# Second layer's query stacks transposed by DMA, maxima split and masks on GpSimd, rounding products on ScalarE

## What is computed

```
x += attention(layernorm(x), context, mask)      # 16 heads; masked scores; softmax over 128 keys; output product
x += feed_forward(layernorm(x))
layer 0: products of rounded activations (127 steps of the row's largest value) and ternary weights; tanh form of silu(gate) * up, rounded again, down
layer 1: gate logits, the best 2 of 8 experts, two fp32 products per expert, weighted sum
```

## Time and profile before

| | |
|---|---|
| time, median of 3 runs | 215.11 us (214.87 to 216.59) |
| the profiled execution's own time | 216.64 us |
| its span, first to last instruction | 214.8 us |
| TensorE (PE) busy | 196.6 us, 92% |
| VectorE (DVE) busy | 162.4 us, 76% |
| ScalarE (ACT) busy | 135.3 us, 63% |
| GpSimd (POOL) busy | 82.7 us, 38% |
| mean granted clock of TensorE | 0.987 of full speed |

### The profile page before, as it was taken

How to read it: one execution, slowest core, us unless ns; L and a number is a source line. 1 busy time by engine, 2 the same in 40 slices (tenths; PEclk the granted TensorE clock), 3 DMA queues, 4 the chain that set the end, 5 groups by cost and what they waited for, 6 DMA issues and landing times.

```text
span 214.8 us, 6119 instructions
## 1 busy us (share of the span) xinstructions
PE 196.6 (92%) x2114; PEld 160.8 (75%) x2114; DVE 162.4 (76%) x608; ACT 135.3 (63%) x378; POOL 82.7 (38%) x197
## 2 busy tenths in 40 slices
PE   2487697999999999999999999999999999999992
PEld 0255474757766777777888988898979889999992
DVE  6458989999999999999987859966576736265225
ACT  3343466468868677766968579547955576566430
POOL 4494320432337544143520425438210604232532
PEclk9999889999999999999999999999999999999998
DMA  5849678504440724430080000400220000000000
GB/s 156 243 111 303 164 98 349 145 9 101 108 92 0 160 50 92 98 87 17 2 92 9 5 0 17 98 3 12 54 47 6 0 15 0 17 0 15 2 10 24
DMA packets 39747, 15.09 MB, mean 70 GB/s; under 512 B 34211, under 2 KB 38819, under 8 KB 39462
## 3 DMA queue, kind: packets, MB, share of 16 engines
q1 hardware_dynamic: 39142, 14.00, 27.7%
q10 hardware_dynamic: 576, 0.72, 1.0%
HBM read 5.80 MB, written 0.52 MB: 29 GB/s over the span
## 4 chain that ended last, share of the span: by engine, by line
PE 81%; DVE 7%; DMA 5%; issue 2%; SPq 2%; POOL 1%; ACT 1%; DVEq 0%; ACTq 0%
PE ps_B L826 14%; PE ps_A L839 12%; PE ps_O L756 7%; PE ps_B L690 7%; PE ps_A L675 6%; PE ps_B L692 6%; PE ps_Q L708 6%; PE ps_A L677 6%; DMA m0T_i<-in_mask0T 5%; PE ps_O L764 3%; PE ps_X L722 2%; PE ps_A L791 2%; PE ps_O L774 2%; PE ps_A L835 2%; PE ps_P L736 2%
## 5 line engine op out<-in xcount | busy, mean ns | idle before, releaser
L907 ACT ACTIVATE probs<-ps_B 128x512 f32<-128x512 f32 x64 | 36.5, 598 | 15.6 <-PE ps_B L692 14.8
L956 ACT ACTIVATE hid<-ps_B,b_sb 128x128 f32<-128x128 f32 x128 | 35.6, 378 | 15.3 <-PE ps_B L826 15.2
L1063 DVE TENSOR_REDUCE mx<-ps_A 128x4 f32<-128x512 f32 x64 | 42.0, 677 | 3.7 <-PE ps_A L677 3.7
L826 PE MATMUL ps_B<-mxT,w_sb 128*128 128x128 f32 x256 | 33.3, 278 | 0.0
L839 PEld LDWEIGHTS ps_A<-w_sb,hid 128*128 128x128 f32 x256 | 31.1, 192 | 0.6
L839 PE MATMUL ps_A<-w_sb,hid 128*128 128x128 f32 x256 | 31.2, 275 | 0.0
L826 PEld LDWEIGHTS ps_B<-mxT,w_sb 128*128 128x128 f32 x256 | 30.6, 192 | 0.5 <-issue 0.4
L654 POOL TENSOR_TENSOR yc<-yc 128x512 f32<-128x512 f32 (+2 forms) x21 | 17.3, 823 | 34.1 <-DVE yc L1228 33.0
L675 PE MATMUL ps_A<-m_b,id_b 128*128 128x512 bf16 x64 | 24.7, 385 | 2.4 <-DVE mx L1063 1.2
L692 PEld LDWEIGHTS ps_B<-qmT,kblk 118*128 118x128 bf16 x256 | 20.4, 100 | 8.6 <-issue 0.8
L692 PE MATMUL ps_B<-qmT,kblk 118*128 118x128 bf16 x256 | 25.5, 223 | 0.0
(11 more groups left out here) (135 smaller groups left out, 391.5 us busy)
## 6 DMA issues: line engine op xcount, KB each, us to landing
w_sb<-in_m1T SPq DMA_DIRECT2D x1, 1024.0 KB, 6.2
w_sb<-in_m2T SPq DMA_DIRECT2D x1, 1024.0 KB, 8.1
out_y<-out_sb SPq DMA_DIRECT2D x8, 64.0 KB, 1.5
x_sb<-in_x SPq DMA_DIRECT2D x1, 448.0 KB, 6.7
ctx_sb<-in_ctxT ACTq DMA_DIRECT2D x1, 448.0 KB, 5.5
m_i<-in_mask SPq DMA_DIRECT2D x1, 384.0 KB, 4.2
m0T_i<-in_mask0T SPq DMA_DIRECT2D x1, 384.0 KB, 5.0
kblk<-kst SPq DMA_TRANSPOSE x16, 3.7
```

The costliest lines, as they stand in the source:

```text
L826: mm = pe.matmul(psum("z", b, i)[:, c * P:(c + 1) * P], w1_sb[:, 4 * i + c, :], mxT[:, b % 2, :], start=True, stop=True)
L907: ends(act.activation(probs[:, n % 2, 4 * i:4 * i + 4, :], psum("exp", n, i)[:, :].rearrange("p (h k) -> p h k", h=4), ACT.Exp, scale=ATTN ...
L956: ins = act.activation(hid[:, b % 2, 4 * i + c, :], psum("z", b, i)[:, c * P:(c + 1) * P], ACT.Relu, bias=b1_sb[:, 4 * i + c:4 * i + c + 1])
L1063: ends(dve.tensor_reduce(mx[:, n % 2, 4 * i:4 * i + 4], psum("max", n, i)[:, :].rearrange("p (h k) -> p h k", h=4), AX.X, ALU.max), "dve.max")
```

## The change

1. In layer 1 the query stack is turned by two DMA transposes on SP's queue (`sp.qs`, `sp.qb`) in place of sixteen TensorE transposes and two ScalarE copies. Layer 0 keeps TensorE. The buffers `qst`, `qT` and `qmT` get 4, 3 and 3 slots (before 3, 2, 2).
2. The split of the maxima runs on GpSimd (`p1`, `pr`, `p2`, `p3`) in both layers; the reduction itself negates its result. The masks of layer 0 are made on GpSimd.
3. The multiply-and-add of the three roundings (`xr`, `hr`, `wa`) runs on ScalarE.
4. The masks are loaded in three pieces (2, 2 and 4 sequences), the expert weights in four pieces each, behind the fourth to seventh key transposes; layer 1's small tensors go one key transpose later.
5. Units (0,6) and (0,7) come ahead of (1,1), and the due times are all new, with six values per unit in place of one. To make room, `th` and `hr` lie in the buffer of the weights, and the bias buffers in `yc`.

```diff
+QSLOTS = 4
+TSLOTS = 3
+MSLOTS = 3
+BY_DMA = (1,)
...
-UNIT_ORDER = ((0, 0), (0, 1), (0, 2), (0, 3), (0, 4), (0, 5), (1, 0), (1, 1), (0, 6), (0, 7), (1, 2),
+UNIT_ORDER = ((0, 0), (0, 1), (0, 2), (0, 3), (0, 4), (0, 5), (1, 0), (0, 6), (0, 7), (1, 1), (1, 2),
...
+QUERY_STACK = ((("pe.qs", 1, "pool.ql"), ("act.qs", 1, "pe.qs")),
+               (("sp.qs", 1, "pool.ql"),))
+SHIFTED_STACK = ((("pe.qb", 1, "pool.p3"), ("act.qb", 1, "pe.qb")),
+                 (("sp.qb", 1, "pool.p3"),))
...
                 if n == 0:
                     sp.dma_start(wo_sb[0][:, :], w0o).then_inc(s_wo, 16)
+                    masks(1, 2, 4)
                 if n == 1:
-                    masks(1, 2, NB)
...
                 if n == 2:
+                    masks(2, 4, NB)
...
+                if n in (3, 4, 5, 6):
+                    part = slice(4 * (n - 3), 4 * (n - 3) + 4)
+                    sp.dma_start(w1_sb[:, part, :], m1T[:, part, :]).then_inc(s_moe, 16)
+                    sp.dma_start(w2_sb[:, part, :], m2T[:, part, :]).then_inc(s_moe, 16)
...
+                if name == "qs":
+                    after(sp, "pool.ql", n)
+                    if n >= TSLOTS:
+                        after(sp, "pe.max", n - TSLOTS)
+                    if b >= 2:
+                        wait_landed(sp, b - 2, "qs")
+                    sp.dma_start_transpose(qT[:, n % TSLOTS, :, :], qst[:, n % QSLOTS, :, :].rearrange("p g c -> p (g c)")
+                                           ).then_inc(landed["qs"][b % 2], 16)
+                if name == "qb":
+                    after(sp, "pool.p3", n)
+                    if n >= MSLOTS:
+                        after(sp, "pe.exp", n - MSLOTS)
...
+                if name == "mk":
+                    if b in (0, 2, 4):
+                        for src in s_mask[b:b + 2]:
+                            pool.wait_ge(src, 16)
+                    pool.tensor_scalar(m0_b[:, b, :], m0_i[:, b, :], 0.0, MASKED, ALU.is_equal, ALU.mult)
+                    ends(pool.tensor_scalar(m0T_b[:, b, :], m0T_i[:, b, :], 0.0, MASKED, ALU.is_equal, ALU.mult), "pool.mk")
+                if name == "p1":
+                    st, m, rest = head_max(n)
+                    after(pool, "dve.max", n)
+                    ends(pool.tensor_copy(st[:, :, :, 0], m), "pool.p1")
+                if name == "pr":
...
+                    ends(pool.tensor_tensor(rest, m, st[:, :, :, 0], ALU.subtract), "pool.pr")
+                if name == "p2":
...
+                    ends(pool.tensor_copy(st[:, :, :, 1], rest), "pool.p2")
+                if name == "p3":
...
+                    ends(pool.tensor_tensor(st[:, :, :, 2], rest, st[:, :, :, 1], ALU.subtract), "pool.p3")
...
+            def query_stack_ready(n):
+                if units[n][0] in BY_DMA:
+                    wait_landed(pe, units[n][1], "qs")
+                else:
+                    after(pe, "act.qs", units[n][1])
...
+                if name == "hr":
+                    after(act, "dve.h3", b)
...
+                    ends(act.activation(hr[:, :], z2[:, b % 2, :], ACT.Copy, bias=ROUND, scale=fs[:, b, 11:12]), "act.hr")
+                if name == "xr":
...
+                    ends(act.activation(xr[:, b % 2, :], fh[:, 0, b % 2, :], ACT.Copy, bias=ROUND, scale=fs[:, b, 3:4]), "act.xr")
+                if name == "wa":
...
-                                           psum("max", n, i)[:, :].rearrange("p (h k) -> p h k", h=4), AX.X, ALU.max),
-                         "dve.max")
...
+                                           psum("max", n, i)[:, :].rearrange("p (h k) -> p h k", h=4), AX.X, ALU.max,
+                                           negate=True), "dve.max")
```

More of the change, by code:

```diff
@@ L118 @@
     ("dve.fn", 1, "pool.fp"),
-)
+) for l in range(2)]
 STEPS = (
-    (("dve.mk", 1),) + ATTENTION + (
+    (("pool.mk", 1),) + ATTENTION[0] + (
         ("dve.q0", 1, "dve.fn"),
@@ L262, in steps_of @@
+GROUP = {name: k for k, names in enumerate(STAGES) for name in names.split()}
 def steps_of(n):
@@ L287, in ready @@
             if n >= ring:
-                needs.append((reader, n - ring, parts[0][reader] - 1))
+                if reader == "stack.qb":
+                    reader = SHIFTED_STACK[UNIT_ORDER[n - ring][0]][0][0]
+                needs.append((reader, n - ring, (parts[0].get(reader) or parts[1][reader]) - 1))
         for ring, reader in LAYER_SLOTS[l].get(name, ()):
@@ L291, in ready @@
                 needs.append((reader, number[l, b - ring], parts[l][reader] - 1))
+        if name in ("sp.qs", "sp.qb") and b >= 2:
+            needs.append((name, number[l, b - 2], 0))
         if name in AFTER_LAYER0 and l == 1:
             needs.append(("dve.dn", number[0, b], 0))
-        if name in AFTER_KEYS and b >= AFTER_KEYS[name][0]:
-            needs.append(("sp.ks", AFTER_KEYS[name][1], 0))
+        needs += [("sp.ks", k, 0) for first, k in AFTER_KEYS.get(name, ()) if b >= first]
         if b == 0:
@@ L412, in build @@
         b1_sb = sb("b1_sb", [P, ZCH])
-        b2_sb = sb("b2_sb", [P, E * P])
-        b2_f = sb("b2_f", [P, E * P])
+        yc = sb("yc", [P, 2, E, P])
+        b2_sb, b2_f = [yc[:, i, :, :].rearrange("p e o -> p (e o)") for i in range(2)]
         b2_h = sb("b2_h", [P, E * P], BF16)
@@ L482, in build @@
         bank_zero, last_out_ready, last_sum = sem("bank_zero"), sem("last_out_ready"), sem("last_sum")
-        ks_landed = [sem("ks_landed0"), sem("ks_landed1")]
+        landed = {k: [sem(f"{k}_landed{i}") for i in range(2)] for k in ("ks", "qs", "qb")}
         s_out = [sem("out_stored0"), sem("out_stored1")]
@@ L885, in _ @@
                     after(act, "pe.q", n)
-                    if n >= 3:
-                        after(act, "pe.qb", n - 3)
+                    if n >= QSLOTS and units[n - QSLOTS][0] in BY_DMA:
+                        wait_landed(act, units[n - QSLOTS][1], "qb")
+                    elif n >= QSLOTS:
+                        after(act, "pe.qb", units[n - QSLOTS][1])
                     elif n:
@@ L1172, in _ @@
                     ends(dve.tensor_scalar(f(11), f(10), QMAX, f(5), ALU.mult, ALU.mult), "dve.h3")
[L1173 to L1177 removed]
                 if name == "hq":
[L1179 removed]
+                    after(dve, "act.hr", b)
                     if b >= 2:
```

276 lines of the change are left out of this document (131 added, 145 removed), and 7 rows, old and new, of the table START.

## The result

The changed kernel is slower: 218.32 us median of 4 runs (217.79 to 220.15) against 214.99 for the kernel before, a ratio of 1.0171 with an interval of 1.0135 to 1.0208. The forecast was 204.4 us, so 13.9 us are to be explained, and the measured time lies outside the forecast's range of 195 to 214.5 us.

The account below looks back on a forecast made before the run. TensorE's work was taken as the bound behind 75 us, with VectorE also near full before. From 216.64 us, -7.2 - 4.3 + 0.8 = -10.7 gave 205.9; less 1.53 to the median, 204.4 us, range 195 to 214.5.

Parts of the forecast that it names:

- 16 stacks off TensorE: Layer 1, nearly all behind 75 us: 16 stacks at 0.45 us leave TensorE, whose work is the time there; -7.2 us.
- VectorE's relief, masks at the start: Ahead of 75 us: VectorE's relief closes TensorE gaps, -4.3 us; first masks on GpSimd delay the start, +0.8 us.
- The new order is not costed: All engines' lists: with TensorE full, a new order can change only gaps already counted; 0 us.
- The second rival: GpSimd paces layer 0: splits waiting for maxima hold the next unit's parts; 214.6 us, no change to measure; chance 0.10.
- The -4.3 ahead of 75 us: Ahead of 75 us: relieving VectorE wins back two thirds of TensorE's recoverable 6.4 us; -4.3 us.
- Its own sign of being wrong: From 20 to 40 us: TensorE still starving, not under 2 us idle, or dropping to the lower clock level.
- the 6.4 us: TensorE's recoverable time before 75 us: idle 3.46 and 1.26 us, plus 1.7 us lost to slow clock at 25 to 29.
- 1.53 us above the median: Whole kernel: the profiled execution's 216.64 us lies 1.53 us above the runs' median; taken off the forecast.
- Landings at 0: Layer 1: query stacks land 0.8 to 2.7 us later by DMA, covered by expert products; 0 us.
- a landing at the front of TensorE's list: TensorE's list: a wait for a landing at its front while expert products stand behind it would show the forecast wrong.
- ScalarE's part near 0: ScalarE: 9.5 us of copies leave, at most 11 us of rounding products come; about even, 0 us.

Follow-up runs that it names:

- run 6: The kernel before with layer 1's sixteen query stacks left out altogether, neither on TensorE nor by DMA, every other step's order unchanged: 212.73 us.
- 15: The changed kernel with GpSimd's list reordered, the bias load one key transpose earlier, and layer 1's sixteen stacks left out altogether: 211.35 us.
- run 11: The changed kernel with seven steps of GpSimd's list in other places and the bias load one key transpose earlier: 212.51 us.
- run 9: The changed kernel with only seven steps of GpSimd's list in other places, no work added or removed: 213.18 us.
- run 2: The changed kernel with layer 1's stacks back on TensorE and ScalarE, all other lists as they are: 221.6 us.
- 7: The changed kernel with layer 1's sixteen stacks left out altogether, no DMA transposes and nothing in their place: 216.95 us.
- run 1: The kernel before with layer 1's query stacks turned by DMA, with 4, 3 and 3 slots, other lists as before: 218.39 us.
- 8: The kernel before with the split of the maxima alone moved to GpSimd, right behind each unit's maxima: 215.43 us.
- run 16: The kernel before with layer 1's stacks left out altogether and the split of the maxima on GpSimd: 212.18 us.
- run 12: The changed kernel with GpSimd's list reordered, the bias load earlier, and four parts of score products moved in TensorE's list: 214.23 us.

## Why the prediction was wrong

The terms of the sum along one path of steps from the kernel before to the changed one, in medians of runs:

| term | forecast | measured | from |
|---|---|---|---|
| 16 stacks off TensorE | -7.2 | -2.3 | before against 6 (215.05, 212.73) |
| VectorE's relief, masks at the start; measured: all else of the change, with GpSimd's list mended | -3.5 | -1.4 | 6 against 15 (211.35) |
| landings of the DMA transposes | 0 | +1.2 | 15 against 11 (212.51) |
| the bias block's place | 0 | +0.7 | 11 against 9 (213.18), ranges overlap |
| the new order of GpSimd's list | 0 | +5.1 | 9 against the changed kernel (218.32) |
| sum | -10.7 | +3.3 | |

A price depends on the lists around it: in the changed ones the stacks on TensorE cost 221.6 - 216.95 = 4.7 us (runs 2 and 7), not 2.3. The rounding products on ScalarE, the loads in pieces, the unit order and the due times were not run by themselves; they are in the -1.4.

- **"The new order is not costed: with TensorE full it can change only the gaps already counted. 0 each."** This step failed by most, 5.1 us for GpSimd's list and up to 5.8 with the bias load, and it turned the sign: run 11 without it lies under the kernel before. Ahead of 75 us TensorE was not full, and the order decides there what it waits for. I priced the work that GpSimd got (1.36 us for two masks, 1.24 for a split; both came out about so) and not its place in a list that is served in order. The second rival named the mechanism ("a split waiting for maxima holds the next unit's parts") and priced it at no change, 214.6 us, 3.7 below what was measured; it had a chance of 0.10. The mask behind such a split is the case.
- **"There TensorE's amount of work is the time" behind 75 us, -7.2 in full.** The work did leave, but run 6 shows that only 2.3 us of it come off when the order of every other step stays. That TensorE was busy for 133.65 of 133.8 us says that it ended last, not by how much: the next chains were 2.3 us behind. The quarter of the stretch that other engines had to spare is no measure of that either, since a chain of dependent steps needs no full engine.
- **The -4.3 ahead of 75 us.** Its own sign of being wrong came: from 20 to 40 us TensorE stands idle for 3.63 us (forecast under 2) at a granted clock of 0.91 (forecast full). Two things were wrong with it. VectorE's relief was 10.0 us, not 22.1, since groups' busy times overlap: from 20 to 75 us VectorE is busy for 46.2 of 55 us, 84%, where the forecast had about 70 (its own rows give 64). And 1.7 of the 6.4 us was the half clock of 25 to 29 us, which the other profiled executions with nearly the same lists there do not have: runs 1, 6, 8 and 16 were granted 1.00 in that stretch. The same execution lay 1.53 us above the median, which I took off too. If the half clock is what set it apart, the two thirds of 1.7 us that are in the -4.3 were counted twice. Where VectorE did come down, from 20 to 40 us, TensorE waited for GpSimd's list in its place. What the relief is worth by itself no run shows.
- **Landings at 0.** Lists that plan for them hide most (1.2 us); lists that do not pay 218.39 - 212.73 = 5.7 us (run 1 against 6, which has fewer slots). The wait that I named as the sign of being wrong, a landing at the front of TensorE's list, is there (2.0 us in two waits), but run 12 shows that moving it back does not win it. The Trainium skill's rule to turn a 128x128 block on TensorE where PSUM will do as the destination (VectorE: DVE Perf Modes, "Rules for kernel authors") is borne out in the old lists, where the DMA is 3.8 us slower (run 1), and not in the changed ones, where it is 3.3 us faster than the stacks on TensorE (run 2).
- **Right:** the work moved (TensorE 190.9 us, GpSimd 108.9), and ScalarE's part near 0: of the waits listed only one of 0.9 us, for `hq`, lies behind a rounding product.

**Still open** is what holds the 4.9 us of the first term. It is not the landings (run 6 has none), and taking the split off VectorE gives at most 0.5 (run 16). Run 6's chain of waits speaks for most of it lying ahead of 114 us, in chains through VectorE. That the order of TensorE's own list keeps it is a guess; a list made anew for the shorter work was not tried.

## What to carry to other kernels

A chain that is all one engine tells who ends last, not how far the next is behind; leave the work out altogether and measure before you book its whole price as a gain. When steps go to an engine that serves a list in order, read what stands behind each of them and what each waits for: here seven steps in another order were worth 5.1 us, more than the 2.3 and 1.4 us that the moves brought. And a disturbance that only the profiled execution shows belongs to its distance from the median, not to the gain.

## What the runs showed of the hardware

**GpSimd steps took three to six times as long beside one VectorE instruction.** The layer-1 mask took 2.16 us and a 16-column cast 1.26 (above, 39.31 and 41.54 us); the same took 0.71 us in the kernel before and 0.22 elsewhere. VectorE meanwhile ran a product and sum of two inputs in SBUF, the on-chip memory:

```profile
39.26 1.26 DVE L1094 SCALAR_TENSOR_TENSOR yc<-b_h,cst_sb,yc 3x1024 f32<-3x1024 bf16 x1
...
41.45 1.25 DVE L1094 SCALAR_TENSOR_TENSOR yc<-b_h,cst_sb,yc 3x1024 f32<-3x1024 bf16 x1
```

Both GpSimd steps began just behind the start of such an instruction, by 0.05 and 0.09 us, and ended after it. In run 9, where no such instruction ran beside it, the mask took 0.66 us. The Trainium skill (SBUF — State Buffer, "Who interferes with whom" and "SBUF: two separate sides") says that VectorE and GpSimd share one pair of ports, and that a VectorE operation with two SBUF inputs and a GpSimd one that reads SBUF block each other: whichever starts first holds the pair for the whole instruction. The trace agrees in its times: the cast ended at 42.80 us, 0.10 us behind VectorE's instruction, and the mask at 41.47 us, 0.95 behind the first one. The block itself is not seen in a trace.

**The price of a DMA transpose grows less than its size.** In the changed kernel eight blocks of 128x128 landed in 3.3 us in the middle case (the shifted stack in 2.8) and took SP 1.24 us to issue; sixteen took 3.7 and 1.63. Twice the blocks thus cost about a third more to issue.
